# Making GpSimd wait for its indirect transfers, group by group, in both expert stages

## The reference, cut to what matters

```python
# first mixture: 8 experts, 2 per token, at most CAP = 512 tokens for each expert
disp = zeros((E, CAP, C)).at[ids_f, pos_c].add(xr * keep)      # tokens gathered by expert
h    = relu(einsum('enc,ech->enh', disp, ew1) + eb1)           # 128 -> 512
eo   = einsum('enh,ehc->enc', h, ew2) + eb2                    # 512 -> 128
y    = eo[ids_f, pos_c] * (probs_f * keep)                     # back to the tokens' order
...
# second mixture: 8 experts, 2 per token, no limit
g    = silu(h1) * h3                                           # h1, h3: 128 -> 256, with low-rank parts
y_e  = _lora_out(g, W2, b2, A2, B2)                            # 256 -> 128
y    = einsum('te,ted->td', gates, y_e)
```

## Time and profile before

| | us |
|---|---|
| median of three runs | 960.75 |
| lowest, highest run | 959.2, 961.38 |
| span of the profiled execution | 1025.8 |
| first experts in it, first gather to last scatter's issue | 454.60 to 551.34 |
| second experts in it, first scatter to last scatter's issue | 862.08 to 995.89 |

### The profile page before, as it was taken

One profiled execution on the slowest core, in us unless ns is written; L12 is line 12 of the kernel. 1 busy time (PEld: TensorE's weight loads), 2 busy tenths in 40 slices (PEclk: granted clock), 3 DMA queues, 4 the chain that ended last, 5 costly groups with the idle time before them and its releaser, 6 DMA issues. The chain is left out here.

```text
span 1025.8 us, 21613 instructions
## 1 busy us (share of the span) xinstructions
PE 741.2 (72%) x6690; PEld 525.1 (51%) x6690; DVE 685.5 (67%) x3220; ACT 456.1 (44%) x1217; POOL 575.1 (56%) x944
## 2 busy tenths in 40 slices
PE   0687889796749999429892279989898756877750
PEld 0344445453736565225561157766666535777650
DVE  6998899887236876761110848977878564777754
ACT  3656665554004554202231747755556214544430
POOL 6788888868355442026663744455655452556550
PEclk9867887867559999768996559988988667999985
DMA  6300114994129785013542300000000016766517
GB/s 130 69 7 9 40 52 87 98 82 59 41 120 288 246 251 161 11 12 67 87 116 74 112 1 4 8 23 21 25 19 24 25 39 200 220 191 203 160 36 246
DMA packets 98690, 93.94 MB, mean 92 GB/s; under 512 B 37497, under 2 KB 82288, under 8 KB 98001
## 3 DMA queue, kind: packets, MB, share of 16 engines
q1 hardware_dynamic: 91126, 78.82, 31.1%
q0 software_dynamic: 6592, 13.58, 5.2%
q10 hardware_dynamic: 858, 0.17, 0.1%
HBM read 47.24 MB, written 43.19 MB: 88 GB/s over the span
## 5 line engine op out<-in xcount | busy, mean ns | idle before, releaser
L2342 POOL DMA_INDIRECT expert_pairs<-e_ys,e_home x78 | 78.9, 1011 | 76.5 <-DVE e_ys L2364 58.1
L1766 POOL DMA_INDIRECT expert_slots<-r_rows,r_slotu x64 | 63.2, 988 | 47.8 <-DVE r_rows L2095 31.7
L1750 POOL TENSOR_SCALAR a_kb<-a_kr,a_m,a_bk 128x128 f32<-128x128 f32 x128 | 57.5, 449 | 49.5 <-ACT a_kr L1963 32.9
L918 DVE MATCH_REPLACE8 work<-m,work 128x64 f32<-128x64 f32 x384 | 75.6, 205 | 0.0
L2309 PE MATMUL e_ps<-e_XH,e_wh 128*128 128x256 f32 x156 | 49.1, 315 | 26.7 <-DVE e_hh L2376 23.4
L1948 ACT ACTIVATE a_pp<-a_dd 128x512 f32<-128x512 f32 x64 | 40.2, 629 | 59.7 <-DVE a_dd L2135 57.2
L1537 POOL DMA_INDIRECT ex_rows<-rows,slot_source x32 | 30.7, 961 | 53.3 <-POOLq L1215 43.9
L905 DVE MAX8 m<-work 128x8 f32<-128x64 f32 x384 | 56.9, 207 | 0.0
L793 PE MATMUL psf<-filmw,us 97*128 97x512 f32 x64 | 51.3, 897 | 1.1 <-ACT FO L814 1.0
L2174 DVE RECIPROCAL a_rt<-a_pso 128x128 f32<-128x128 f32 x31 | 29.5, 953 | 30.7 <-PE a_pso L1876 21.3
L1591 ACT ACTIVATE ex_hs<-ex_psh,vec 128x512 f32<-128x512 f32 x32 | 20.9, 687 | 65.4 <-remote 36.2
(11 more groups left out here) (443 smaller groups left out, 2388.1 us busy)
## 6 DMA issues: line engine op xcount, KB each, us to landing
expert_slots<-rt_unfilled SPq DMA_DIRECT2D x151, 130.0 KB, 2.9
e_wf<-folded_weights SPq DMA_DIRECT2D x39, 386.0 KB
e_xr<-expert_slots SPq DMA_DIRECT2D x39, 130.0 KB
planes<-rt_zeros SPq DMA_DIRECT2D x4, 1024.0 KB
ew<-in_L_ffn_ew SPq DMA_DIRECT2D x16, 256.0 KB
comb_y<-planes SPq DMA_DIRECT2D x16, 256.0 KB, 5.7
pair_y<-expert_pairs SPq DMA_DIRECT2D x16, 256.0 KB, 5.8
folded_weights<-fold_done SPq DMA_DIRECT2D x8, 384.0 KB, 4.1
```

The source lines that it names most:

```text
L918: return own.did(dve.match_replace(wk_[x.j][:, h, :], m8[x.j][:, h, r, :], src[:, h, :], TAKEN))
L1750: m = pool.tensor_scalar(kb[a.j][:, :, h, :], k, m4[:, h:h + 1], bk4[:, h:h + 1], ALU.mult, ALU.add)
L1766: pool.indirect_dma_start(G.slots, bass.IndirectOffsetOnAxis(ap=slot[:, b, k, t:t + 1], axis=0), rb[b % NB][:, k, t, :], None).then_inc(se ...
L2342: pool.indirect_dma_start(G.pair, bass.IndirectOffsetOnAxis(ap=home[i % NY][:, k:k + 1], axis=0), ys[i % NY][:, k, :], None).then_inc(kept ...
```

## The change

GpSimd gets three waits more. In the first experts, before the scatters of expert `e`, it waits until the youngest gather that it has issued has landed (`fetch(e + 3)`, or `fetch(7)` from `e` = 4 on); and before each `fetch(e + 4)` it waits until the scatters of expert `e` have landed. In the second experts, before the two scatters of tile `i`, it waits until those of tile `i - 1` have landed. Nothing else changes: the same transfers, the same buffers, the same order.

```diff
@@ first_experts, GpSimd
                 for e in range(NE):
                     j = e % 2
                     pool.wait_ge(s["y_sb"], e + 1)
+                    last = min(e + AHEAD, NE) - 1
+                    pool.wait_ge(rows[last % AHEAD], (last // AHEAD + 1) * S * 16)
                     for k in range(S):
                         pool.indirect_dma_start(G.planes, bass.IndirectOffsetOnAxis(ap=G.home[:, S * e + k:S * e + k + 1], axis=0),
                                                 ys[j][:, k, :], None).then_inc(kept[j], 16)
                     if e + AHEAD < NE:
+                        pool.wait_ge(kept[j], (e // 2 + 1) * S * 16)
                         fetch(e + AHEAD)
@@ second_experts, GpSimd
                 for i in range(NTILE):
                     pool.wait_ge(s["y_sb"], i + 1)
+                    if i > 0:
+                        pool.wait_ge(kept[(i - 1) % NY], ((i - 1) // NY + 1) * S * 16)
                     for k in range(S):
                         pool.indirect_dma_start(G.pair, bass.IndirectOffsetOnAxis(ap=home[i % NY][:, k:k + 1], axis=0),
                                                 ys[i % NY][:, k, :], None).then_inc(kept[i % NY], 16)
```

## The result

The changed kernel took 1078.52 us, the median of four runs (1073.07 to 1084.89), against 960.16 us for the kernel before (959.2 to 961.38): a ratio of 1.121, 95% interval 1.116 to 1.127, 118 us slower. I had forecast 1037, with 1062 as the upper end. The direction and the mechanism held; the size did not.

A forecast was written before the change was run, and what follows sets the result against it. No engine was full before; GpSimd, waiting for its own transfers, would bound the second experts. 960.75 us plus 14 for the first experts and 62 for the second gave 1036.8, forecast 1037 us, own range 1015 to 1062, full range 994 to 1062.

The forecast's parts named there:

- The chain that bounds: Second experts: with the added wait nothing overlaps a tile's landing, so GpSimd becomes the bound at 4.2 us a tile.
- The clock the sum is made against: Both expert stages: gaps come with the profile's recording and are not in timed runs; 42.4 of 65 us.
- the gaps of before: Late TensorE signals in the earlier profile, every second tile in the second experts: 33.7 us there, 8.7 in the first experts.
- Rival A: Both expert stages: the gaps are in the timed runs too, giving 994 us; chance 0.11.
- The sign that I had named: Whole kernel: the profile's span grows much less than the runs' median, their difference shrinking from 65 to about 22 us.
- A tile of the second experts: GpSimd's issues 2.41 us plus landing and wake-up 1.8 make 4.2 us a tile against 2.57, +62 us in the runs.
- the sign of a mis-sized landing: Second experts: a tile taking under 3.75 or over 4.8 us would show that the landing was mis-sized.
- The first experts: Four scatter waits of 1.5 us and four gather waits of 3.5 on GpSimd add 14 us in the runs.
- My row: First experts: the trace's first gathers, 3.68 us from the fourth issue's end to TensorE's start, used to price gather waits.
- rival B: Second experts: TensorE's clock falls to 1.2 GHz, or a landing takes 2.7 us under load, 5.1 a tile, 1071 us; chance 0.08.
- The kernel that the Trainium skill tells of in the prediction: Cited under the clock rival for TensorE in the second experts: a kernel whose clock fell at every such wait.
- Everything else untouched: All other stages, their order and transfers stay as before, and the two expert stages' shifts add up.

The follow-up runs named there:

- the first part alone: Only the first experts' waits, for gathers before scatters and for scatters before the next fetch, added to the kernel before: 981.16 us, ratio 1.020.

## Why the prediction was right or wrong

**The chain that bounds.** Right. GpSimd became the bound of the second experts, VectorE waits there for scatters, and 37 of 38 tiles start when the tile before has landed.

**The clock the sum is made against.** The choice was right, the reason wrong. I priced the gaps of before at 33.7 and 8.7 us; the unchanged kernel without them is 34.9 and 8.8 us shorter in the two stages, and its first experts take 87.9 us where I had worked out 88.0. But I put them down to the recorder. They came in timed runs too, in two of the five sets of runs, where the kernel before takes 1040 us. Rival A (gaps in the timed runs) is what happens there: it gave +33 us, and 65 was measured, short mainly by the same term as below. That the runs of the forecast were of the kind without gaps is therefore luck in part. The sign that I had named came: the profile's span grew by 58 us, the median by 118, and the difference between them shrank from 65 to 5 us (I had said 22).

**A tile of the second experts: the step that failed.** I had 2.41 + 1.8 = 4.2 us; measured were (186.1 - 2.2) / 38 = 4.84, above the 4.8 that I had named as the sign of a mis-sized landing. Three of its terms were off. The issues behind a wait on a transfer take 2.22 us, not 2.41. Landing and wake-up without load take 2.01 us, not 1.5: the bytes have gone 0.9 us after the issue as in the earlier trace rows (the issue ends at 1011.08 in the changed kernel, and the engines are all but quiet from 1011.80 on),

```profile
1011.60:1011.80 0.20, 0.20 (x3) 0.20 (x3) 0.00 (x0) 0.20 (x1) 0.00 (x0) 0.50 0.90 307
1011.80:1012.00 0.20, 0.20 (x3) 0.20 (x3) 0.00 (x0) 0.20 (x1) 0.00 (x0) 0.50 0.10 21
```

and the rest is 1.1, not 0.57. Part of that is GpSimd's own: for one and the same landing VectorE starts 0.65 us earlier (its address calculation in the timeline of the changed kernel),

```profile
982.52 0.17 DVE L2365 TENSOR_SCALAR e_away<-e_xr 128x2 f32<-128x2 uint32 x1 [2.36 <-DMA expert_pairs<-e_ys,e_home]
```

against GpSimd's 983.17. I had taken the wake-up, 0.27 us, from a wait for VectorE. And the transfers that share the engines, the weights' above all, add 0.6 us a tile on average, not 0.3. Over 38 tiles: the unloaded tile 4.23 against my 3.9, 13 us; the loads, 11 us. Together 24 of the 25 us between 62 and the measured 87 us. I had held that the loads slow down with the tiles and so matter less. They slowed down (DMA share 0.43 in the stage) and fell in step with the scatters, and the landing was longer all the same.

**The first experts.** +14 predicted, 17.7 and 20.7 measured. The scatters' wait was right to 0.03 us (1.53 in the changed kernel against 1.5). The gathers' was 3.5, from one row; measured were 5.06, 5.45, 3.92 and 2.62 us, 4.3 on average, in the whole change (the first ended by VectorE's signal). Four times 0.8 is 3 us, nearly all of the 3.7 that are missing. My row was that of the first expert, and the waits differ from expert to expert; why was not tried. By the Trainium skill (DMA: Bandwidth & Descriptors, section Anatomy of one DMA) 64 KB would have landed 2.15 us after the start of the issue and the stage come to +6, both estimates from the page's fit. The trace does not agree: behind four gathers in a row it is 0.95 + 4.3 = 5.2 us on average until GpSimd goes on, and my own row was too low as well.

**TensorE's clock, rival B.** The clock fell again and again in the second experts after the change, to 0.89 on average from 905 to 1008 us, but not throughout, and GpSimd's chain hid it: a tile took 4.93 us at the full clock and 4.96 at 0.67. The kernel that the Trainium skill tells of in the prediction waits about 3 to 5 us in each round; here TensorE waited 1.6 us on average (31.1 us in 19 waits of that stretch), and its clock fell in some tiles only. Rival B's time, 1071 us, came close, by another cause: its alternative, a landing of 2.7 us under load, is what loaded tiles show (2.8 with the wake-up, over 28 tiles). I had given it 0.08 and left it out of my range.

**Everything else untouched.** Not quite: this term stood at nothing in my sum. The work between the two expert stages took 305.4 us in the profile of the whole change against 288.7. The second attention in it, the same stretch of 810 to 840 TensorE instructions, changed kernel and then unchanged kernel:

```profile
674.00:726.00 52.00, 48.98 (x844) 38.61 (x844) 41.34 (x117) 31.53 (x82) 34.02 (x56) 0.80 0.07 23
```

```profile
654.00:699.00 45.00, 40.35 (x812) 31.15 (x801) 42.53 (x121) 31.46 (x84) 33.91 (x56) 1.00 0.09 27
```

TensorE is nearly full there in both, and it had the full clock in one and 0.80 in the other. Other kernels whose code between the stages is the same showed 288.1, 288.6 (twice), 291.9, 299.7 and 301.6 us where the gaps were absent. One of the two at 288.6 is the first part alone, whose code up to the second experts is that of the whole change; and where the gaps were there, the whole change took 322.2 us and the others 314.8 to 328.4. So the change alone does not bring it about. The sum of the two stages is 87.2 + 17.7 = 105 us; the other 13 of the 118 are probably of this kind. Whether the change makes the slower clock likelier there stays open: one profile is too few to tell. Of the 42 us between the 76 that I forecast and the 118, the tile thus makes 25, the first experts 4 and this 13.

## What to carry to other kernels

A wait of the issuing engine for its own transfer turns a throughput into a latency: each round then costs issue plus landing plus wake-up, so the cost is the number of rounds times what isn't covered, and it is zero as soon as enough rounds lie between the transfer and the wait (three tiles of 2.5 us here). Price such a landing with the wake-up of the engine that waits and under the loads that go out beside it; the same signal may release them. And compare a profiled execution with the median of the runs before pricing a gap: one that is 65 us longer can show a state that the runs were not in, and a change can be worth half as much there.

## What the runs showed of the hardware that was not expected

- GpSimd starts an indirect transfer 0.65 us after VectorE starts on the same landing; behind a wait for a VectorE result it is 0.27 us.
- An indirect scatter of 64 KB, alone on the engines, is through 0.9 us after its issue ends, and GpSimd goes on 2.01 us after it. Four gathers of 64 KB in a row need 2.6 to 5.8 us behind the last issue.
- In some sets of runs, timed runs too, the engines that wait for TensorE go on up to 2 us after the trace shows its work as done, every second tile: the kernel before takes 960 us in some sets and 1040 in others. In the profile of before ScalarE, which waits for another product, goes on at the same moment as VectorE in the earlier trace rows (915.30):

```profile
915.34 0.38 ACT L2325 ACTIVATE e_XH<-e_pst 128x256 fp32r<-128x256 f32 x1 [2.21 <-DMA cs<-in_ctx]
```

  Whether the signals are late, as the prediction has it, or the matmuls themselves, whose ends are modelled in the trace, no run tells apart. The record has chip 1 for a set of either kind, so it is not a matter of which chip; what causes it was not tried.
